# Unread products in TensorE's waits: a perceiver block on one core of a Trainium2

## What is computed

```python
x = x + xattn(layernorm(x), ctx_1024, mask, Wq, Wkv, Wo, qn_w, kn_w)   # 32 x 257 context rows, 8 heads of 64, q and k normalised per head
x = x + attn(layernorm(x), ...)     # sigmoid projections, weights from spike-time differences, no softmax
x = x + ffn(layernorm(x), gate_w, w1, w2, w3)
# ffn: scores = softmax(xf @ gate_w); the 2 best of 8 experts per token
#      xs = scale * xf; h = silu(xs @ w1) * (xs @ w3); out = sum over experts of h @ w2
```

## Time and profile before

| | |
|---|---|
| median of 3 runs | 788.39 us (788.24 to 789.43) |
| the profiled execution, its own time | 791.38 us |
| its span in the trace | 789.60 us |
| TensorE matmuls busy | 748.8 us (95%), 4501 instructions |
| VectorE, ScalarE, POOL busy | 552.7, 494.8, 238.8 us |
| mean granted TensorE clock | 0.977 |

### The profile page before, as it was taken

The page is one execution under the profiler, slowest core; times in us unless marked ns, Lnnn a source line. Parts: engine busy times, 40 slices in busy tenths (PEclk is TensorE's granted clock), DMA queues, the critical chain, the costliest instruction groups (busy, mean ns, idle before and its releaser), DMA issues.

```text
span 789.6 us, 13562 instructions
## 1 busy us (share of the span) xinstructions
PE 748.8 (95%) x4501; PEld 653.6 (83%) x4501; DVE 552.7 (70%) x1046; ACT 494.8 (63%) x1089; POOL 238.8 (30%) x182
## 2 busy tenths in 40 slices
PE   4898999999999999999999998999999958999996
PEld 3687899899999898998999997988788856877875
DVE  6877886776867868867868776885567754555573
ACT  4666786785867768767858666556465423655650
POOL 2562212121211212121212113842860002555545
PEclk9999999999999999999999999999999957999999
DMA  8841211212121211212121302661106472566658
GB/s 299 86 120 41 66 57 41 81 48 72 40 80 40 80 40 58 61 40 80 41 79 41 112 22 52 178 211 54 54 1 214 145 284 78 96 110 109 106 77 319
DMA packets 59671, 75.18 MB, mean 95 GB/s; under 512 B 8784, under 2 KB 33360, under 8 KB 59632
## 3 DMA queue, kind: packets, MB, share of 16 engines
q1 hardware_dynamic: 52032, 58.16, 24.8%
q0 software_dynamic: 4720, 11.27, 7.9%
q10 hardware_dynamic: 2880, 5.24, 1.8%
HBM read 54.75 MB, written 19.92 MB: 95 GB/s over the span
## 4 chain that ended last, share of the span: by engine, by line
PE 83%; DVE 7%; DMA 3%; ACT 3%; issue 2%; POOL 1%; SPq 0%; POOLq 0%; ACTq 0%; DVEq 0%
PE pK L32 38%; PE pV L32 14%; PE pP L32 11%; PE pS L32 6%; PE pT L1700 3%; PE pT L1519 3%; PE pP L1683 2%; DMA big<-x_rows,idx_x 1%; PE pT L1814 1%; DMA fin<-total 1%; PE pT L1499 1%; PE pS L1768 1%; DVE bst L976 1%; DMA total<-big,idx 1%; DVE head_mean L996 1%
## 5 line engine op out<-in xcount | busy, mean ns | idle before, releaser
L32 PE MATMUL pK<-parts 128*128 128x512 f32 x840 | 210.5, 398 | 0.7 <-POOL parts L547 0.7
L516 POOL TENSOR_TENSOR parts<-big,parts 128x1024 fp32r<-128x1024 f32 x32 | 77.3, 2416 | 338.8 <-ACT parts L741 338.8
L32 PEld LDWEIGHTS pK<-parts 128*128 128x128 f32 x840 | 152.3, 189 | 29.2 <-POOL parts L547 1.1
L32 PE MATMUL pK<-w,lhs 128*128 x276 | 71.5, 410 | 1.8 <-DVE lhs L1436 1.4
L32 PEld LDWEIGHTS pK<-w,lhs 128*128 128x128 f32 x276 | 51.9, 194 | 13.5 <-issue 3.5
L1018 DVE TENSOR_TENSOR kn<-pK,head_rs 128x512 f32<-128x512 f32 x62 | 42.6, 688 | 20.1 <-ACT head_rs L643 19.5
L1452 DVE TENSOR_TENSOR w_p<-big,w_p 128x1024 fp32r<-128x1024 f32 x22 | 27.0, 1226 | 39.5 <-ACT w_p L933 39.5
L769 ACT ACTIVATE pT<-pP 128x512 fp32r<-128x512 f32 x32 | 19.1, 598 | 55.6 <-PE pP L1683 55.6
L32 PE MATMUL pS<-kT,qblk 128*128 128x258 f32 x384 | 51.4, 284 | 2.0 <-DVE qoT L1052 2.0
L32 PE MATMUL pP<-pT,parts 128*128 128x256 f32 x384 | 53.0, 288 | 0.0
L32 PEld LDWEIGHTS pP<-pT,parts 128*128 128x128 f32 x384 | 47.6, 192 | 3.5
(11 more groups left out here) (320 smaller groups left out, 1638.2 us busy)
## 6 DMA issues: line engine op xcount, KB each, us to landing
big<-in_ctx_dram SPq DMA_DIRECT2D x32, 512.0 KB, 3.8
total<-zero SPq DMA_DIRECT2D x32, 256.0 KB, 4.0
w_raw<-in_L_ffn_w_dram SPq DMA_DIRECT2D x16, 512.0 KB, 5.6
big<-in_L_ffn_w_dram SPq DMA_DIRECT2D x8, 512.0 KB, 7.6
fin<-total SPq DMA_DIRECT2D x8, 512.0 KB, 7.2
big<-in_L_xattn_Wkv_dram SPq DMA_DIRECT2D x2, 1024.0 KB, 11.0
x_rows<-big ACTq DMA_DIRECT2D x8, 256.0 KB, 2.1
total<-big ACTq DMA_DIRECT2D x8, 256.0 KB, 2.4
```

Of the source, the lines that this page charges most:

```text
L32: last = pe.matmul(out, lhs(a, c), rhs(b, c), start=start and c == first and n == 0, stop=stop and c == chunks - 1 and n == 2)
L516: nc.gpsimd.tensor_tensor(ctxN[:, u, LO], ctx_raw[:, u], ctxN[:, u, HI].bitcast(F32), ALU.subtract).then_inc(cn_lo, 1)
```

## The change

A helper `keep_pace(n, bank, weights)` issues n matmuls of 128x512 from split weights that lie in the memory already, into a PSUM bank that nothing reads until it is written anew. Each starts and stops its own sum, none increments a semaphore. It is called at five places on TensorE. One gate product is moved. No other engine's instructions change.

```diff
+            def keep_pace(n, bank, weights):
+                for _ in range(n):
+                    pe.matmul(bank, weights[:, 0:P], weights, start=True, stop=True)
+
             def batch(tile, r, main=True, prev=True, nxt=True, first=False):
...
+                if first:
+                    keep_pace(7, pV1[:, :], wkv[:, HI, 0, D:2 * D])
                 if prev:
                     pe.wait_ge(k_lo, b * MT)
...
                     project(1)
+                if main and not nxt:
+                    pe.wait_ge(sc_m, b)
+                    keep_pace(6, pS[:, 0, :], wkv[:, HI, 0, D:2 * D])
                 if prev:
                     pe.wait_ge(p_n, b * G)
...
+                if s == TILES + 1:
+                    gate_product(TILES - 2)
                 t = s - 2
                 if 0 <= t < TILES:
                     ln_turn(2 * TILES + t)
                 t = s - 3
-                if t >= 0:
+                if t >= 0 and t != TILES - 2:
                     gate_product(t)
 
+            pe.wait_ge(w13_lo, 1)
+            keep_pace(10, pKV[0][:, :], w13[:, 0, HI, 0])
             pe.wait_ge(member_set, 1)
             pe.matmul(p_count, before_bf[:, :], member[:, :, :], start=True, stop=False)
...
             last.then_inc(n_mm, 1)
+            keep_pace(18, pKV[0][:, :], w13[:, 0, HI, 0])
             pairs = TOP_K * TILES
...
+            keep_pace(6, pKV[0][:, :], w13[:, 0, HI, 0])
             pe.wait_ge(expert_set, 1)
             slot_turn(0)
```

## The result

The changed kernel takes 792.42 us (median of 11 runs, 789.79 to 794.41); the kernel before took 789.23 us beside it (11 runs, 787.27 to 790.33). The ratio is 1.0043, with a 95% interval of 1.0027 to 1.0058: +3.4 us, between +2.1 and +4.6. Forecast were 788.7 us and a range up to 790.9.

What follows compares the result with a forecast made beforehand. TensorE alone was taken to bound the loop over the batches, with its clock low at the last batch and in routing. Terms 1.6 - 1.0 + 0.8 + 1.0 + 0 - 1.7 - 0.4 = +0.3 us gave 788.7 us, range 786.6 to 790.9.

Steps and rivals of the forecast that it cites:

- Term 1: First scores: seven fills stand behind the wait for the last query tile and delay the scores by their length, +1.6 us.
- Term 2: Last batch: six fills fit the wait, keep the clock up and let twelve 128x256 products end sooner, -1.0 us.
- Rival (c): Last batch: timed runs of before did not lose the clock there, term 2 is 0, sum +1.3, 789.7 us; chance 0.15.
- Term 3: Last gate products: the moved product pushes the last turn and no longer covers the copy's time, +0.8 us.
- Terms 4 to 7: Routing and first slot: ten, eighteen and six fills, summed as +1.0 + 0 - 1.7 - 0.4 = -1.1 us.
- 4: Ahead of the counts: ten fills run at 1.2 GHz and outlast the wait, +1.0 us.
- 5: After the counts: eighteen fills bring the clock back early and fit the 5.55 us wait, 0.
- Term 6: Slot-number products: sixteen at full clock take 1.9 us in place of 3.59, -1.7 us; six later fills have room.
- Term 7: First slot: clock expected to fall again before its hidden product, so only -0.4 us of a possible -2.7.
- the same: Whole kernel: a time of 786.8 to 790.0 us, within about 0.2% of no change; chance 0.62.
- Rival (a): Routing: clock does not return before the slot-number products, terms 6 and 7 are 0, +2.4, 790.8 us; chance 0.17.
- The rule of the Trainium skill: First slot: transposes do not count as TensorE busy, so it starts at half clock; term 7 is 0, sum +0.7.

Runs made afterwards that it cites:

- e5_routing: Kernel before with only routing's ten, eighteen and six fills, gate product not moved: ratio 1.0004, +0.3 us.
- e16_no_gate: Changed kernel with the gate product back in its old place, all 47 fills kept: ratio 1.0022, +1.7 us against the kernel before.
- e6_no_first: Changed kernel without the seven fills of the first batch: ratio 1.0016, +1.3 us against the kernel before.
- e11_seven_early: Changed kernel with the seven fills moved ahead of the wait for the last query tile: ratio 1.0004, +0.3 us against the kernel before.
- e4_gate: Kernel before with only the second last gate product moved ahead of the last turn: ratio 1.002, +1.6 us.
- e1_first7: Kernel before with only the seven fills of the first batch, behind the wait for the last query tile: ratio 1.0024, +1.9 us.
- e9_all_waits: Kernel before with seven fills ahead of the query-tile wait, six at last batch, six before last turn, ten, eighteen, twelve in routing: 0.9975, -2.0 us, 787.14 us.
- e15_five: As e9_all_waits with five fills in place of the twelve ahead of the first slot: ratio 0.9992, -0.6 us against the kernel before.
- e12_safe: As e9_all_waits but three fills before the last turn, six before the counts, twelve after, four before the first slot: 0.9996, -0.3 us against kernel before.
- e8_eighteen6: Kernel before with only the eighteen fills after the counts and the six ahead of the first slot: ratio 0.9990, -0.8 us.
- e13_pad20: Kernel before with 20 tiny unread float32 products in the wait after the counts, no fill: ratio 1.0004.

## Why the prediction was wrong

The sum was +0.3 us and it is +3.4. The profiles, cut into stretches, show where the time went (us; the means are over one profile each of the kernels that have nothing changed in the stretch, their number in brackets; the third row's six include the two with tiny products, and the last row's are those with fewer than 34 fills):

| stretch | nothing changed there | changed kernel |
|---|---|---|
| end of the wait ahead of the first scores to the last keys | 409.2 to 411.2, mean 410.1 (9) | 412.6 |
| last keys to the 24 output products | 12.2 to 13.2, mean 12.9 (9) | 12.2 |
| second layer's first output product to the turn behind the first slot's hidden product | 65.3 to 68.2, mean 66.6 (6) | 67.9 |
| first final product to the end | 19.0 to 19.5, mean 19.3 (10) | 21.4 |

In the third row routing's fills without the moved gate product give 64.9 and 65.0 (e5_routing, e16_no_gate) and with it 66.6 to 67.9 (e6_no_first, e11_seven_early, the changed kernel). By terms:

- **Term 1, seven fills, +1.6: right.** +1.9 alone (0.9 to 2.9), by position and not by length, as the order of instructions had shown. Missed was that the clock can fall as the fills begin behind this wait: they took 1.88, 2.78 and 3.21 us in three profiles. The same fall costs the scores when there are no fills, so what the fills add is near the full-clock price either way, 1.4 and 1.6 us.
- **Term 2, the last batch, -1.0: this step failed.** The size was right for the profiled execution (0.9 us). But it was put on the median of the timed runs, and three of nine profiles never lose the clock there. Rival (c) named this and had 0.15. Measured +0.4 (-0.6 to 1.4): 1.4 us of the miss.
- **Term 3, the gate product, +0.8: right in sign and mechanism.** +1.6 alone (0.5 to 2.7), 1.7 within the whole; +0.8 lies inside the first interval, so that it was too small is not shown by the times. The steps (input 0.1 us ahead of the turn's, then the copy uncovered) are in the timeline with 1.54 and 0.75 us. From where the turn could have started to the end of the last gate product the traces give +0.8 us with the clock down (5.1 in e6_no_first, 4.3 before) and +1.0 with it up most of the time (3.5 in e4_gate, 2.5 in e1_first7). What may come on top is the clock: it fell early enough to lengthen the gate products in all four profiles with the product moved and in four of ten without, and a fall is worth up to 1.9 us here. From the second layer's first output product to the counts are 43.3 us where it stays up, 44.9 to 45.2 where it falls with nothing changed, 44.3 with the product moved and 46.0 to 47.2 with it moved and the ten fills behind it. Four profiles are few, and this part is not shown.
- **Terms 4 to 7, routing, -1.1: what failed is that a cost at the end of the kernel was put at nothing.** Measured +0.3 (-1.1 to 1.7, so the forecast lies at the very end of the interval). In their own stretch the fills did what the sum gave them, 64.9 and 65.0 us against a mean of 66.6. But no term has the final stretch, which is 1.0 us longer in the kernels with 34 fills or more, and 2.1 us longer than the other kernels' mean in the changed kernel's profile. Of the single terms, 4 measured +1.0 (-0.4 to 2.4) and 5 held in the whole. Term 6 was over-sized: at a clock of 1.00 throughout (e5_routing, e9_all_waits, e15_five, e16_no_gate) the sixteen take 2.2 us behind a wait and not 1.9, and in the changed kernel, where the clock falls on the way, 2.79. The six fills, priced at nothing with room to spare, ran at 1.2 GHz there and held the first turn up by 0.7 us. In e5_routing and e16_no_gate they ended in time, and the rows came late beside the loads of w2. Term 7 cannot be told from one profile: with nothing changed ahead of it the first slot's hidden product takes 4.3 to 5.5 us in six profiles, with the ten, the eighteen and the six 4.6 to 4.9 in three and 3.0 in two.
- The forecast's "the same" had 0.62 and "slower" 0.20. Rival (a), +2.4, came out nearest in size and for another reason: the clock did come back before the slot-number products. What was wrong besides was the method: each term was priced from one execution at the clock of that one, in a kernel whose clock at these places differs from run to run. That execution had lost the clock at the last batch and from the last turn on, and its third stretch is 68.2 us, at the long end of the six.

The rule of the Trainium skill that was weighed ("TensorE: Matmul & The Clock Gate", PE-mode transpose) would have given +0.7 in place of +0.3. With the changed kernel's fills the first slot did start at half clock behind two turns, 4.63 us, in agreement with it; in e6_no_first it ran 3.02 us and in e9_all_waits 3.04 us behind the same two turns. e6_no_first has the same instructions ahead of these turns as the changed kernel, so neither the rule nor what stands there settles the term: it differs from execution to execution, and by what is open.

## What to carry to other kernels

A product that only keeps the clock must stand ahead of the wait that it is to fill: look which instruction carries the semaphore, for behind it every fill is added in full. Look whether the clock is already down where fills are to go, as each takes 0.45 us there and not 0.23. Counting them so that they fit even then was no remedy here, though: e12_safe did that and measured -0.3 us, e9_all_waits with more fills -2.0. Do not move real work into a wait whose input comes as late as the waiting one's. And before a fall of the clock is priced, look at several executions for how often it happens.

## What the runs showed of the hardware

- Waits of 1.48 and 0.57 us with twelve turning matmuls between and behind them were enough to lose the clock in six of nine profiles. Behind the one of 2.0 us ahead of the first scores it was lost in four of nine without fills (the twelve scores took 2.3 to 2.8 us in place of 1.7).
- Matmuls back to back do not keep the clock up by themselves: in the changed kernel the 16 products of 24 columns, without a gap between them and behind a wait of 1.03 us, went from full clock to half on the way. In e8_eighteen6, right behind the eighteen fills without a wait, they and the next sixteen stayed at 1.00 (1.85 and 1.94 us), so the wait may have its part in it.
- Adding 34 fills brought one block of instructions more on queue 8 (0.38 for 0.36 MB), 24 fills did not. The Trainium skill ("Runtime: NRT & Kernel Launch", instruction fetch mechanics) gives blocks of 16 KiB, 256 instructions; the trace agrees, one packet and 0.02 MB for at least 68 instructions, and e13_pad20 shows no cost of it that could be measured (+0.3 us, -1.2 to +1.8).
